# Gated attention with a routed mixture of experts: another order for the first loads, and the second batch's row statistics one step later

## What is computed

```python
def reference(x, w_qkv, b_qkv, w_out, b_out, router_w, router_b,
              expert_w, expert_b, proj_w, proj_b, norm_w):
    xn = layernorm(x)                                    # eps 1e-5, no weights
    # attention, one head of width 512
    q, k, v = split(xn @ w_qkv.T + b_qkv)
    s = softmax(q @ k.T / sqrt(512)) @ v @ w_out.T + b_out
    # mixture of experts, top 2 of 8
    top_vals, top_idx = top_k(xn @ router_w + router_b, 2)
    gate = softmax(top_vals)                             # scattered to 8 columns
    h = silu(einsum('td,edf->etf', xn, expert_w) + expert_b)
    y = xn + (sum_e gate_e * h_e) @ proj_w + proj_b
    g = silu(norm_w * y / rms(y))
    return x + s * g
```

## Time and profile before

| What | us |
|---|---|
| median of 3 runs | 490.99 |
| the three runs | 490.71, 490.99, 493.17 |
| time of the profiled execution | 490.71 |
| its span in the profile | 489.0 |
| TensorE busy in it | 478.2 |
| first matmul starts at | 4.44 |

### The profile page before, as it was taken

One profiled execution on the slowest core, in us unless ns is written; L12 is line 12 of the kernel. 1 busy time (PEld: TensorE's weight loads), 2 busy tenths in 40 slices (PEclk: granted clock), 3 DMA queues, 4 the chain that ended last, 5 costly groups with the idle time before them and its releaser, 6 DMA issues.

```text
span 489.0 us, 7145 instructions
## 1 busy us (share of the span) xinstructions
PE 478.2 (98%) x2146; PEld 388.1 (79%) x2147; DVE 312.5 (64%) x474; ACT 207.7 (42%) x300; POOL 205.4 (42%) x289
## 2 busy tenths in 40 slices
PE   6999999999999999999999999999999999999995
PEld 3688787888888888878888888878888878888884
DVE  2657152578632436979888888762597754857762
ACT  1265463143331154736444444322655441644550
POOL 2145210005887859703000000744568873377234
PEclk9999999999999999999999999999999999999999
DMA  8764999966888599897996666897555864445512
GB/s 309 272 238 166 379 382 369 390 207 227 294 294 304 188 334 304 252 295 205 262 282 202 195 200 184 310 305 267 158 156 170 264 192 147 138 158 170 172 47 84
DMA packets 77630, 115.77 MB, mean 237 GB/s; under 512 B 6608, under 2 KB 36320, under 8 KB 77600
## 3 DMA queue, kind: packets, MB, share of 16 engines
q1 hardware_dynamic: 63872, 77.62, 50.4%
q0 software_dynamic: 7440, 25.45, 14.7%
q10 hardware_dynamic: 6288, 12.33, 7.1%
HBM read 66.09 MB, written 49.28 MB: 236 GB/s over the span
## 4 chain that ended last, share of the span: by engine, by line
PE 92%; DVE 3%; DMA 2%; issue 2%; SPq 0%; ACT 0%; DVEq 0%
PE ab L1589 20%; PE ab L1590 20%; PE ab L1591 20%; PE sc L1589 7%; PE sc L1591 7%; PE sc L1590 7%; PE sc L1605 3%; PE tp L1595 2%; DMA xg<-rows_scratch 2%; PE tp L1639 2%; DVE y L1468 1%; PE sc L1668 1%; DMA raw_v<-in_w_qkv 1%; PE ab L1613 1%; PE sc L1671 1%
## 5 line engine op out<-in xcount | busy, mean ns | idle before, releaser
L781 POOL DMA_INDIRECT y<-y_scratch,pos x32 | 33.3, 1042 | 88.8 <-DMA y_scratch<-yt_so 74.2
L1589 PE MATMUL ab<-W,st_h 128*128 x156 | 60.8, 390 | 0.6 <-DVE st_l L1297 0.6
L1591 PE MATMUL ab<-W,st_l 128*128 x156 | 60.7, 389 | 0.0
L1590 PE MATMUL ab<-W,st_h 128*128 x156 | 60.7, 389 | 0.0
L764 POOL DMA_INDIRECT rows_scratch<-xb,pos x32 | 31.2, 974 | 51.0 <-DVEq L1285 42.8
L1589 PE MATMUL sc<-xt_h,t_h 128*128 128x512 f32 x128 | 50.1, 391 | 0.0
L1591 PE MATMUL sc<-xt_h,t_l 128*128 128x512 f32 x128 | 49.8, 389 | 0.0
L1590 PE MATMUL sc<-xt_l,t_h 128*128 128x512 f32 x128 | 49.8, 389 | 0.0
L1026 ACT CAST st_h<-tp 128x512 fp32r<-128x512 f32 x39 | 22.9, 587 | 41.1 <-PE ab L1591 39.0
L1353 DVE TENSOR_REDUCE small<-sc 128x1 f32<-128x1024 f32 x16 | 19.5, 1222 | 24.3 <-PE sc L1591 21.9
L1589 PEld LDWEIGHTS ab<-W,st_h 128*128 128x128 f32 x156 | 29.3, 188 | 7.1 <-issue 1.0
(11 more groups left out here) (270 smaller groups left out, 1197.2 us busy)
## 6 DMA issues: line engine op xcount, KB each, us to landing
rows_scratch<-xn ACTq DMA_DIRECT2D x3, 3328.0 KB, 20.2
xb<-in_expert_w POOLq DMA_DIRECT2D x6, 1024.0 KB
xn<-rows_scratch SPq DMA_DIRECT2D x48, 128.0 KB, 3.4
xg<-rows_scratch SPq DMA_DIRECT2D x44, 128.0 KB
y_scratch<-yt_own SPq DMA_DIRECT2D x20, 256.0 KB, 3.1
y_scratch<-yt_so SPq DMA_DIRECT2D x19, 256.0 KB, 2.9
p_scratch<-prob SPq DMA_DIRECT2D x9, 512.0 KB, 2.9
rows_scratch<-xs SPq DMA_DIRECT2D x16, 256.0 KB, 5.9
```

Of the source, the lines that this page charges most:

```text
L781: pool.indirect_dma_start(y[:, q, :], None, y_d, bass.IndirectOffsetOnAxis(pos[:, GB * s + p:GB * s + p + 1], 0))\
L1589: nc.tensor.matmul(dst, lh, rh, start=start, stop=False)
L1590: nc.tensor.matmul(dst, lh, rl, start=False, stop=False)
L1591: return nc.tensor.matmul(dst, ll, rh, start=False, stop=stop)
```

## The change

Four things are altered.

- SP now issues for each chunk c, in this order, `raw_v`, `raw_o` and two tiles of x; ACT no longer issues `raw_o`.
- ACT issues `bcols` and behind it `bo_bc`, both on `vec_in`, and the first DVE instruction waits for both (32 where it was 16).
- POOL issues the router's weights and bias without the wait for `x_in[2]`, and no longer issues `bo_bc`. The wait for `rw_in` on DVE moves from `fold_value_bias` to `fold_biases`, with 32 for 48.
- The row statistics of batch 1 on DVE go from the steps t = 2 to 5 to the steps t = 3 to 6.

```diff
-            for c in range(KC + 1):
-                if c < KC:
-                    sp.dma_start(raw[2][:, c, :], wqkv_v[2][:, c, :]).then_inc(vo_in[c], 16)
-                if c >= 1:
-                    w = slice(2 * c - 2, 2 * c)
-                    sp.dma_start(xb[:, w, :], x_v[0][:, w, :]).then_inc(x_in[c - 1], 16)
+            for c in range(KC):
+                sp.dma_start(raw[2][:, c, :], wqkv_v[2][:, c, :]).then_inc(vo_in[c], 16)
+                sp.dma_start(raw[3][:, c, :], wout_v[:, c, :]).then_inc(vo_in[c], 16)
+                w = slice(2 * c, 2 * c + 2)
+                sp.dma_start(xb[:, w, :], x_v[0][:, w, :]).then_inc(x_in[c], 16)
...
-            pool.wait_ge(x_in[KC - 2], 16)
...
-            pool.dma_start(bo_bc, b_out.rearrange("(a n) -> a n", a=1).to_broadcast([P, D])).then_inc(rw_in, 16)
...
-            for c in range(KC):
-                act.dma_start(raw[3][:, c, :], wout_v[:, c, :]).then_inc(vo_in[c], 16)
             act.dma_start(bcols[:, :, :], b_qkv).then_inc(vec_in, 16)
+            act.dma_start(bo_bc, b_out.rearrange("(a n) -> a n", a=1).to_broadcast([P, D])).then_inc(vec_in, 16)
...
-            dve.wait_ge(vec_in, 16)
+            dve.wait_ge(vec_in, 32)
...
             def fold_value_bias():
 
-                dve.wait_ge(rw_in, 48)
                 dve.wait_ge(vecs, 1)
...
             def fold_biases():
 
+                dve.wait_ge(rw_in, 32)
                 dve.wait_ge(const, 6)
...
-                if 2 <= t < 6:
-
-                    n = t - 2
+                if 3 <= t < 7:
+
+                    n = t - 3
```

## The result

The changed kernel took 494.23 us (median of 17 runs, 492.11 to 495.53), the kernel before 490.99 (median of 17 runs in the same comparison, 489.87 to 493.74). The ratio is 1.0054 with a 95% interval of 1.0037 to 1.0072, so the change costs 2.7 us by the ratio and 3.2 by the medians. Predicted were 492.0 us and a range of 490.8 to 493.6. The profiled execution of the changed kernel took 495.23, with a span of 493.5.

The account below looks back on a forecast made before the run. The prediction took TensorE, busy 478.2 of 489.0 us, as the bound; start 0.1, transposes stall 1.0 and logit_rows 0 summed to 1.1 us later, a median of 492.0, with an 8 in 10 range of 490.8 to 493.6.

Parts of the forecast that it names:

- The start, 0.1 us later: Opening: TensorE's first matmul, waiting for chunk 0 of raw_v and raw_o, 0.1 us later, bounds -0.36 and +1.26.
- upper bound of 1.26: Opening: raw_o landing as late as the second raw_v, which held that place on SP, a start 1.26 us later.
- the packet count: Opening: packets ahead of raw_o's end, begun at 227 per us, put the start between unchanged and 0.5 us later.
- (c): Opening: raw_o, second on SP, lands 1.26 us later; with the stall the sum is 2.3, 493.2 us; chance 0.10.
- (b): logit_rows of batch 1: stores of tiles 8 and 9 land later, a 1.7 us stall joins, 493.8 us; chance 0.11.
- The rule on the rings: Opening: engines alternate between SP's and ACT's rings; raw_v and raw_o mostly precede the bias, term 0 or slightly below.
- No stall in the rest of the opening: Opening after the start: later weight chunks and x tiles stay covered, the tiles by 3.5 us of slack; cost nothing.
- The stall at the transposes, 1.0 us: Transposes of tiles 8 and 9: POOL's later statistics make ACT 1.24 us late; less 0.21 slack, TensorE stalls 1.0 us.
- Nothing at logit_rows: logit_rows of batch 1: slack of 0.32 us just fits if stores land as fast as before; 0 us.
- The clock (d): First weight loads: clock rising one load earlier or later shifts 0.4 us; deciding alone, or anything making it faster, chance 0.04.
- The sum: Whole kernel: 0.1 + 1.0 + 0 = 1.1 us later, median put at 492.0 us.

## Why the prediction was wrong

**The start, 0.1 us later: wrong, and the failed step.** In the changed kernel and in its variants with the broadcast second on ACT the first matmul came at 7.86, 7.34, 7.53, 6.99 and 7.37 us, 2.5 to 3.4 later than before, outside the upper bound of 1.26. The step that failed is the packet count. It took the rate of ordinary loads, 227 packets per us, for packets that all read the same 2 KB; what was begun between 3.6 and 4.44 us was 49 packets, 58 per us. With 128 different rows it was 187 again; with the bias put back, when SP's queue is alone, it was 82. The upper bound was drawn from the second raw_v, also an ordinary load. The broadcast's packets took about twice as long as ordinary ones or more, 26 us of the engines' time for 0.27 MB against 12 (21 to 33 in the five profiles). The term that the prediction put at 0.1 was 2.5 to 3.4.

The trace of the kernel before could not have told this. In it POOL issued the broadcast at 15.07, and it landed 5.6 us later, behind cover. These are its windows, in the columns of the earlier trace rows, and below them the same two windows of the kernel with the bias put back on POOL:

```profile
16.00:18.00 2.00, 2.00 (x6) 1.47 (x5) 1.66 (x11) 0.00 (x0) 0.00 (x0) 1.00 1.05 389
18.00:20.00 2.00, 2.00 (x6) 1.40 (x6) 1.78 (x6) 0.91 (x2) 0.00 (x0) 1.00 0.95 279
...
16.00:18.00 2.00, 2.00 (x6) 1.39 (x6) 1.58 (x4) 0.00 (x0) 0.00 (x0) 1.00 1.06 391
18.00:20.00 2.00, 2.00 (x6) 1.43 (x5) 1.66 (x11) 0.79 (x2) 0.00 (x0) 1.00 1.03 381
```

The fall from 389 to 279 GB/s looks like the mark of the broadcast, but in the lower pair the broadcast moves in the same window at 381. In the upper one 91 of the 291 packets are smaller than 2 KB, those of the router's loads among them, and SP's loads run out. The queue of POOL moved from 13 to 21 us:

```profile
q0 software_dynamic: 144, 0.28, 11.5%
```

That is 0.115 x 8 x 16 = 15 us of the engines' time for 0.28 MB, and 11 us for 0.26 MB in the kernel with the bias put back: the price of different rows. The same row read for 128 partitions was thus not slow there. POOL's queue moved it in larger packets (80 for 0.26 MB, 3.3 KB each) and later; which of the three, the queue, the packets or the time, makes the difference is open, and so is why. The kernel with raw_o on ACT, where ACT's queue moved the broadcast behind raw_o, lies between: from 9 to 14.5 us its packets took 13 us of the engines' time, but from 10 to 11 us all queues together moved only 202 GB/s, at a share of 0.65.

**Which rival came near.** (c), a late start, names the right place with the wrong cause and half the size or less, 1.26 for 2.5 to 3.4. Its price came from raw_o's place on SP, and the runs with the bias put back show that the place costs nothing (4.41). The total of (b), 493.8, is the nearest to 494.23, but by luck, since its wait at logit_rows did not come.

**The rule on the rings.** By the rule cited from the Trainium skill, "DMA: Bandwidth & Descriptors", section "Queues, rings and completion order", an engine takes turns between the queues. The prediction drew from it that raw_o would mostly go ahead of the bias. That doesn't follow: the bias has only the small bcols before it on its queue and raw_o has raw_v, so by turns the bias would come first. With loads of different rows raw_o was all the same little delayed (start at 4.39 to 5.13). With the broadcast it landed 0.3 us behind the bias, which had been issued 0.05 before it. How long a turn is, no run shows.

**No stall in the rest of the opening: right.** TensorE has no wait at its second chunk of weights. The later x tiles (first normalised tile at 21.82 + 0.55 = 22.4 instead of 19.4) were covered, because TensorE itself came later. In the run with raw_o on ACT the same cover ran out.

**The stall at the transposes, 1.0 us: right in place, cause and size.** ACT was to be 1.24 us late; it was 59.55 - 55.95 = 3.60 late, 2.42 of which came from the opening, which leaves 1.18. POOL's wait took the place of the issue of zeros, as said. TensorE lost 0.59 + 0.33 = 0.9 in the changed kernel and 0.9 with the edit alone. By the ratios the edit alone costs 0.7 and 1.2 us, with intervals that just include zero.

**Nothing at logit_rows: right.** No such wait is in any of the lists of TensorE's waits.

**The clock (d): its share is open.** The opening's 32 weight matmuls took 15.92 us instead of 16.92, so that of 3.4 us of late start 2.4 reached the first transposes (25.33 against 22.91). The granted clock reads 1.00 in both; only the spacing of the weight loads, 0.85 us first and 0.42 later, shows the two levels. It changed at 12.0 in the changed kernel and at 10.5 in the kernel before. That this is the doing of the later start is not shown, because the moment moves by itself. These are the loads behind the change, first in the two runs of the statistics alone, which start at 4.44 and 4.48, like the kernel before, then in the second run of the changed kernel with the statistics early, which starts at 7.37:

```profile
8.72 11.04 PEld L1605 LDWEIGHTS sc<-raw_o,raw_v 128*128 128x128 f32 x26 [0.35 <-issue]
8.58 11.04 PEld L1605 LDWEIGHTS sc<-raw_o,raw_v 128*128 128x128 f32 x26 [0.17 <-issue]
...
13.30 10.18 PEld L1599 LDWEIGHTS sc<-raw_o,raw_v 128*128 128x128 f32 x24 [0.28 <-issue]
```

The first run of that last kernel starts at 7.34 and changes at 10.7. The same opening took 15.85 to 16.92 us in the one kind and 15.58 to 16.82 in the other, so a single profile of it is uncertain by over 1 us. The Trainium skill, "TensorE: Matmul & The Clock Gate", Part 1, says that the moment does not follow the first matmul; the trace agrees, with 8.6 to 10.6 for starts at 4.4 and 10.7 to 13.3 for starts at 7.3. The prediction had rival (d) too small: it gave it 0.4 us either way, and two executions "don't show much of it". The runs with TensorE busy from 1.06 us shortened the opening, to 14.12 and 15.07 us for the same matmuls.

**The sum.** Between the two profiled spans lie 4.5 us. The late start accounts for 3.4, less 1.0 in the opening, the transposes for 0.9, st_l and pt_l for 0.5 each and t_l for 0.3, 4.6 in all. The last three are not explained by the change; in the second profile of the changed kernel st_l and pt_l are missing, the start is at 7.0, and its span is 490.7, 1.7 above before. With more profiles the sum rests on firmer ground: the five with the broadcast second on ACT have their first transposes at 24.47 to 25.74, 24.96 on average, and the three with the opening of the kernel before at 21.89 to 22.91, 22.27 on average. That is 2.7 us, and 3.6 with the 0.9 at the transposes, where the changed kernel's two medians say 3.2 and 2.9 and its ratios 2.7 and 3.4. The prediction's own addition is off by 0.1: 490.99 + 1.1 is 492.1, not 492.0.

## What to carry to other kernels

The price of a load that broadcasts one row of HBM to all partitions doesn't follow from its bytes alone. Here it was that of ordinary loads late and on POOL's queue, and some twice that early and on ACT's, where it held up the weights on the other queue. A load of this kind is best put where nothing urgent is in flight, and the time of a queue's packets beside its bytes is the first thing to read for it; the total rate alone misled here. When a step is moved by one place in a loop, follow its last consumer to the cover that hides it; here the cover was an issue that blocked ACT, and it was 2.0 us for a move of 3.2. And where several runs of one kernel differ by 4 us, a wait in the profile tells more about a microsecond than the medians do, but the length of a whole stretch needs more than one profile.

## What the runs showed that I had not expected

- One row of 2 KB read 128 times on ACT's queue in the opening kept the DMA engines busy (share 0.97) at 191 GB/s, where 128 different rows moved at 356 and 1.01, and slowed the loads of the other queue as well: raw_o took 5.6 to 6.4 us to land, against 3.0 with the broadcast put back.
- The same row on POOL's queue, near 18 us, cost no more than different rows: 381 GB/s at 1.03 with the bias put back.
- Up to 8 reads of a row cost the engines little: 12.8, 13.5 and 13.9% of their time with 1, 4 and 8 reads, 22.6 to 35.5% with 128.
- In three profiles of the same opening, with starts at 4.4 to 4.5, the spacing of the weight loads changed anywhere from 8.6 to 10.5 us, so that the same 32 matmuls took 15.85 to 16.92 us.
- Seven small matmuls during an idle start took 1.7 to 2.7 us off the following opening, and the span was 1.2 shorter.
